# Message multiplies of a graph layer joined to 512 columns, with a second addition of the halves

## The reference

```python
def _L0_gnn_ref(node_repr, weight, bias, edge_index, edge_types):
    h_all = jnp.einsum('ni,roi->rno', node_repr, weight)      # 8 relations, 256 x 256 each
    msgs = h_all[edge_types, src]
    messages = jax.ops.segment_sum(msgs, dst, num_segments=node_repr.shape[0])
    return messages + bias
...
x = x + _L0_gnn_ref(_layernorm(x), ...)
x = x + _L0_ffn_ref(_layernorm(x), ...)    # softmax gate, top 2 of 16 experts, silu(x w1) * (x w2) w3
```

## Time and profile before

| what | value |
|---|---|
| median of 3 runs | 1306.32 us (1300.31 to 1306.45) |
| the profiled execution's own time | 1302.33 us |
| its span, first to last instruction | 1300.6 us |
| PE busy | 845.9 us, 65% |
| POOL busy | 670.0 us, 52% |
| DVE busy | 607.5 us, 47% |
| ACT busy | 345.9 us, 27% |
| mean granted TensorE clock | 0.789 of full speed |

### The profile page before, as it was taken

How to read it: one execution, slowest core, us unless ns; L and a number is a source line. 1 busy time by engine, 2 the same in 40 slices (tenths; PEclk the granted TensorE clock), 3 DMA queues, 4 the chain that set the end, 5 groups by cost and what they waited for, 6 DMA issues and landing times.

```text
span 1300.6 us, 19171 instructions
## 1 busy us (share of the span) xinstructions
PE 845.9 (65%) x4904; PEld 689.7 (53%) x4905; DVE 607.5 (47%) x1597; ACT 345.9 (27%) x397; POOL 670.0 (52%) x621
## 2 busy tenths in 40 slices
PE   1256677766677766677666677437897988897600
PEld 1134455555555545555555556326786877786500
DVE  6655454445555444444545555674333333333432
ACT  4502223333222222222333323312222222222100
POOL 1366455554555555545555452056444477738373
PEclk9967777777777777777877777658998988999855
DMA  9523333333333222232222321316625364454244
GB/s 223 168 88 107 102 97 102 103 105 108 118 96 96 77 77 76 76 90 69 77 77 77 88 69 33 117 51 224 202 73 185 97 196 158 150 194 109 82 132 124
DMA packets 93629, 145.98 MB, mean 112 GB/s; under 512 B 13367, under 2 KB 67595, under 8 KB 93610
## 3 DMA queue, kind: packets, MB, share of 16 engines
q0 software_dynamic: 25968, 70.94, 18.9%
q1 hardware_dynamic: 50794, 59.48, 14.3%
q10 hardware_dynamic: 16848, 15.34, 3.6%
HBM read 109.90 MB, written 33.98 MB: 111 GB/s over the span
## 4 chain that ended last, share of the span: by engine, by line
PE 22%; issue 19%; DVE 18%; another core or an unknown queue 16%; ACT 8%; DVEq 7%; DMA 5%; POOL 4%; ACTq 1%; SPq 0%; POOLq 0%
PE ps L1387 6%; PE ps L1265 5%; ACT part L634 5%; PE ps L1369 4%; DVE part L909 4%; PE ps L1253 4%; DVE hot L877 3%; DMA y_tab<-ffn 3%; DVE store L895 3%; DVEq L895 2%; POOL x_sb L556 2%; POOL store L567 1%; PE ps L1395 1%; ACT hot L592 1%
## 5 line engine op out<-in xcount | busy, mean ns | idle before, releaser
L486 POOL DMA_INDIRECT got<-x_tab,idx x425 | 405.2, 953 | 379.2 <-DVE idx L897 237.8
L1253 PE MATMUL ps<-hot,got 125*128 125x256 f16 x1700 | 296.5, 328 | 135.8 <-issue 125.1
L1253 PEld LDWEIGHTS ps<-hot,got 125*128 125x128 f16 x1700 | 187.6, 115 | 236.5 <-issue 187.6
L895 DVE TENSOR_TENSOR store<-store,ps 128x512 f32 x150 | 102.8, 685 | 293.2 <-remote 151.0
L1265 PE MATMUL ps<-part 128*128 128x256 f32 x1152 | 191.2, 341 | 24.8 <-DVE part L909 24.8
L1265 PEld LDWEIGHTS ps<-part 128*128 128x128 f32 x1152 | 186.4, 251 | 27.4 <-DVE part L909 27.3
L1387 PE MATMUL ps<-part,operands 128*128 x696 | 183.6, 415 | 1.2 <-DVE operands L1142 1.2
L1387 PEld LDWEIGHTS ps<-part,operands 128*128 128x128 f32 x696 | 134.0, 199 | 28.3 <-issue 1.8
L909 DVE SCALAR_TENSOR_TENSOR part<-store,part 128x256 fp32r<-128x256 f32 x192 | 103.0, 613 | 66.6 <-ACT part L634 42.1
L619 ACT ACTIVATE dev<-mv,eps 125x1 f32<-125x1 f32 x25 | 7.4, 294 | 474.0 <-DVE mv L924 474.0
L1369 PE MATMUL ps<-part,operands 128*128 x696 | 103.4, 301 | 39.1 <-DVE operands L1152 34.5
(11 more groups left out here) (198 smaller groups left out, 743.7 us busy)
## 6 DMA issues: line engine op xcount, KB each, us to landing
store<-in_L_ffn_w SPq DMA_DIRECT2D x48, 512.0 KB
xs_tab<-x_sb SPq DMA_DIRECT2D x16, 512.0 KB
y_tab<-ffn SPq DMA_DIRECT2D x9, 896.0 KB
ffn<-xs_tab ACTq DMA_DIRECT2D x59, 128.0 KB
y_tab<-ffn ACTq DMA_DIRECT2D x58, 128.0 KB
got<-x_tab,idx POOLq DMA_INDIRECT x425
acc<-in_x SPq DMA_DIRECT2D x5, 560.0 KB
x_tab<-got SPq DMA_DIRECT2D x5, 560.0 KB
```

The source lines that it names most:

```text
L486: nc.gpsimd.indirect_dma_start(got[:, c, :], None, x_tab, bass.IndirectOffsetOnAxis(ap=idx[:, c:c + 1], axis=0)).then_inc(gathered[c], 16)
L895: v.tensor_tensor(window, window, ps[:, WIN_BANK[g], :].rearrange("p (k n) -> p k n", k=KT), ALU.add).then_inc(win_added, 1)
L1253: last = mm(ps[:, WIN_BANK[g], k * KEYS:(k + 1) * KEYS], got[0:CE, c, a * DIM + k * P:a * DIM + (k + 1) * P], hot[0:CE, g % HOT, c - c0, : ...
```

## The change

The multiplies high x high and high x low have the same left operand. They become one multiply of 512 columns, whose right operand is the high and the low part of the weights, one behind the other: the first half of the bank gets high x high, the second high x low. The third product, low x high, is added to the second half. A tile so has 16 multiplies of 512 columns and 16 of 256, 32 for 48, each with its own weight load. The two halves are then both added to `acc`: `add_tile` has a second addition, which waits for the first through a new semaphore. Counted in the instructions that PE issues, its loop body has 237 for 269.

```diff
+        high_added = sem("high_added")
...
             def add_tile(n, tile, bank=MSG_BANK):
                 dve.wait_ge(tile_summed, n + 2)
-                v.tensor_tensor(tile_at(acc, tile), tile_at(acc, tile), ps[0:TP, bank, 0:DIM], ALU.add).then_inc(acc_added, 1)
+                v.tensor_tensor(tile_at(acc, tile), tile_at(acc, tile), ps[0:TP, bank, 0:DIM], ALU.add).then_inc(high_added, 1)
+                dve.wait_ge(high_added, n + 1)
+                dve.sem_inc(stats2_begun, 1)
+                v.tensor_tensor(tile_at(acc, tile), tile_at(acc, tile), ps[0:TP, bank, DIM:], ALU.add).then_inc(acc_added, 1)
                 dve.wait_ge(acc_added, n + 2)
                 dve.sem_inc(stats2_begun, 1)
                 v.bn_stats(stat2[0:TP, :], tile_at(acc, tile)).then_inc(stats2_raw, 1)
...
+                both = ps[:, bank, :].rearrange("p (h d) -> p h d", h=2)
                 for r in range(RELS):
                     for k in range(KT):
-                        for a, b in PARTS:
-                            last = mm(ps[:, bank, 0:DIM], (high, low)[a][:, k, r, :], wT[:, b, k, r * DIM:(r + 1) * DIM],
-                                      start=(r == 0 and k == 0 and a + b == 0), stop=(r == RELS - 1 and k == KT - 1 and a == 1))
+                        mm(both, high[:, k, r, :], wT[:, :, k, r * DIM:(r + 1) * DIM],
+                           start=(r == 0 and k == 0), stop=False)
+                        last = mm(ps[:, bank, DIM:], low[:, k, r, :], wT[:, 0, k, r * DIM:(r + 1) * DIM],
+                                  start=False, stop=(r == RELS - 1 and k == KT - 1))
                 last.then_inc(tile_summed, 1)
```

## The result

The changed kernel takes 1315.55 us, the median of 5 runs (1314.28 to 1318.16), beside 1305.49 for the kernel before (5 runs, 1300.31 to 1306.45). The ratio is 1.0085, with a 95% interval from 1.0065 to 1.0105: some 10 us slower, where +13.4 was predicted. The profiled execution has a span of 1312.9 us for 1300.6.

A forecast was written before the change was run, and what follows sets the result against it. The prediction took a ring through POOL, DVE and ACT to bound the turns, with PE's signals held during POOL's gathers. Second addition 13.7 less 0.3 for joined multiplies gave +13.4 us: 1317 us, range 1311 to 1325.

The forecast's parts named there:

- What holds PE: In the turns, PE's completions come through slowly during POOL's gathers, the held ones after; PE's own work there is worth 0.
- the ring: Repeating chain through POOL's gathers, DVE's additions and ACT's take; pieces sum to 30.10 us a turn, without slack.
- Joined multiplies: PE's 32 multiplies for 48: 0 in the turns, -0.3 us in the uncovered last tile, between 0 and -0.5.
- The shorter list ahead of the signal: g1's signal stands behind 44 pairs of PE instructions for 60: 0 a turn, far bound -0.5 us a turn.
- a fixed rate of 0.57 us a pair: Assumed pace of PE's completions, multiply with weight load, during POOL's gathers; 38 or 36 pairs left need about 20 us.
- the hold: Stretch when PE's completions come slowly: from 2 us after the run's first gather to 3.8 after its last, 14 us.
- price of sooner signals: Rival: the shorter list lets PE's held signals through sooner, -0.5 x 22 = -11 us against +13.7, about 1308 us; chance 0.14.
- Instruction blocks: PE's instruction fetches in the loop: q8 is silent there, so no fetch to save, 0; elsewhere a microsecond either way.
- The second addition: DVE's new addition in add_tile, between g1 and g2: 0.57 us in 24 places, 13.7 us, between 9.8 and 18.5.
- The sum: Whole kernel: 13.7 - 0.3 = +13.4 us, forecast 1317 us, +0.9%, chance 0.70.

The follow-up runs named there:

- the plain copies: Kernel before with each of POOL's indirect gathers replaced by a plain copy of 128 fixed rows of the same table: 1104.01 us, one run.
- the two-additions kernel: Kernel before with the second addition to acc, products kept apart except the first (47 multiplies): 1318.36 us, ratio 1.0102.
- the join alone: Changed kernel with its 32 multiplies, but only the first half of the bank added to acc: 1301.51 us, ratio 0.9970 against the kernel before.
- 28 pairs: Changed kernel without the product low x high, 16 multiplies a tile for 32, both additions kept: 1313.03 us, ratio 1.0047 against the kernel before.
- The body across two blocks: Changed kernel with PE's loop head at slot 128 for slot 0 of a 256-instruction block: 1316.51 us, ratio 1.0072 against the kernel before.

## Why the prediction was right

**What holds PE.** Right: from outside, and PE's work not on the ring. Shown by the plain copies (1104 us, unplaced share 1% for 16%) with PE's program unchanged, and by PE's 28 gapless multiplies after the change that moved the addition of g1 by 0.08 us only (0.12 as the median). The semaphore events add that the signal is raised late, 7 to 10 us after its multiply, and not merely seen late by DVE. That it is POOL's indirect gathers holds for the chips with 1305 us; the third chip runs the same gathers and holds nothing. "PE's work is not on the ring" holds for the order of this kernel; with `messages` behind the run's start it came onto it.

**Joined multiplies.** Mis-sized, by little. In the last tile they start at 824.35 and are through at 832.73, 8.38 us for 8.53: -0.15, where I took -0.3. The first multiply, and the stretches of PE there, the granted clock being the third number from the end:

```profile
824.35 0.79 PE L1269 MATMUL ps<-part,operands 128*128 128x512 f32 x1 [3.98 <-DVE operands L910]
...
825.00:829.00 4.00, 4.00 (x15) 3.41 (x14) 2.90 (x8) 0.70 (x2) 0.00 (x0) 0.50 0.00 0
830.00:832.00 2.00, 2.00 (x13) 1.77 (x12) 0.81 (x2) 0.00 (x0) 0.00 (x0) 1.00 0.00 0
```

PE had been idle 3.98 us and runs the first half at 0.50 (1.2 GHz), 0.64 us for 512 and 256 columns, the second at full clock, 0.35. Before, in the same place, a multiply of 256 columns starts every 0.213 us at 0.50 and every 0.118 at full clock, three of them 0.64 and 0.35. The joined pair takes the same at either level: the columns set the time, and they stayed the same. The -0.3 had come from the expert stage's 0.14 us for 256 columns, which these multiplies don't take.

**The shorter list ahead of the signal.** The forecast was 0 a turn, with -0.5 as the far bound. The signal for g1 came 0.08 us sooner in the turn shown and 0.12 in the median. The turn differs by 0.10 between the two-additions kernel and the full change and by 0.06 between before and the join alone, so by 2.3 and 1.4 us in 22 turns; the lag's 0.12 would be 2.6, of which the odd turn at 236.46 takes back 1.1. The join as a whole gave 3.9 us (2.5 to 5.5 by its interval) and I had 0.3: this is the term that was too small, and 1 to 2 us of it I can't place in the trace. The reasoning behind it stands less well than its number. It took a fixed rate of 0.57 us a pair (the 8.51 us span 14 steps from start to start, so 0.61), it took PE's starts for what is signalled, and it took a fixed end of the hold. After the change all 32 message multiplies and 28 window multiplies had started by 461.15, 6 us ahead of g1's event, so the starts don't tell what is signalled. The counts were rough too: 3.4 us after `messages` begins 18 of its multiplies had started before and 11 after, where I had about 22 and 8. With 28 pairs the signal of g1 came 0.83 us after the last gather, sooner as the rate says, but the signal of g2 then came later, and with `messages` moved behind the gathers' start the signal of g1 came 3.3 us later, with PE's own work in it. So the "price of sooner signals" in the rivals, 0.5 us or more a turn, was not earned by either of the shorter lists that were run, 44 pairs or 28.

**Instruction blocks.** Right. The body across two blocks costs nothing that the runs show (1.0072, 1.0055 to 1.0089, for 1.0085), and a packet more or less on q8 is all. The Trainium skill, "Runtime: NRT & Kernel Launch", section on instruction fetch mechanics, has a taken branch stall when its target lies outside the current window of two pages. The run across two blocks shows no stall and no packet for one; whether its branch leaves that window can't be told from it.

**The second addition.** Right within 0.01 us: 0.56 us between the additions in the trace, 0.56 a turn in the run that has it alone, +13.3 us in all for 13.7. That nothing in the ring had slack for it is shown by the turn, which grew by the same 0.56. It is a right step and no luck: the turn, the pieces and the run that has the addition alone agree. The cover that was there to be used lay elsewhere, ahead of g1, in 11.9 us of idle DVE.

**The sum.** 13.3 for the addition and -3.9 for the join are +9.4; measured were +10.1 by the medians and +11.1 by the ratio (8.5 to 13.7), where the prediction had +13.4. That 1317 lies only 1.5 us from 1315.55 is in part luck: the rise was put 3.3 us too high by the medians, and the start, 1317 - 13.4 = 1303.6, was 1.9 us below the median before.

## What to carry to other kernels

Read a ring before counting an engine's savings: here 16 multiplies fewer, 32 instructions with their weight loads, were worth 3.9 us in a stage of 670, and one addition of 0.41 us on the ring took 13.3. When a change makes a result ready sooner, look who waits for it and move that consumer to where it is idle: the same two additions ahead of g1's turned +0.85% into -1.5%. And where an engine's work ends long before its signal is acted on, replace the suspected disturber by a harmless twin of the same size before tuning the engine itself.

## What was not expected of the hardware

On the chips with 1305 us PE's signals are held while POOL works off a run of indirect gathers: finished sums of g1 (started from 457.72, 12 multiplies of 28 in 3.43 us) have their semaphore event at 467.33 and are acted on at 467.81, and with plain copies in their place the whole kernel takes 1104 us for 1306. One chip didn't do this: it ran the kernel before in 1061 us where the others took 1305 to 1306, and the four runs traced on it, none of them of the kernel before, have turns of about 22 us. Why chips differ is open, and so is which part of a gather causes the hold. A kernel tuned on one kind is tuned for a bound that the other doesn't have.
